# Where the score maxima of two context-attention stages read their queries and keys, and how the query stack is filled

## What is computed

```
x = x + attend(q = adaLN(x) Wq + bq, k, v = adaLN(ctx) Wkv + bkv) Wp + bp          # L0
x = x + gate_a * attend(q, k, v = modulate(LN(x)) W_qkv + b_qkv) W_proj + b_proj   # self
x = x + attend(q = LN(x) W_qc + b_qc, k, v = LN(ctx) W_kvc + b_kvc) W_cproj + ...  # cross
x = x + gate_m * (gelu(modulate(LN(x)) W_mlp1 + b_mlp1) W_mlp2 + b_mlp2)           # mlp, 2048 wide
attend = softmax(q k^T / sqrt(32)) v, for each of the 16 heads
```

## Time and profile before

| | before |
|---|---|
| time, median of 3 runs | 2688.05 us (2682.69 to 2695.44) |
| the profiled execution: its own time | 2690.8 us |
| its span, first to last instruction | 2688.9 us |
| mean granted clock of TensorE | 0.939 |
| busy shares | PE 92%, PEld 64%, DVE 51%, ACT 38%, POOL 21% |
| DMA | 349.15 MB, mean 130 GB/s |

### The profile page before, as it was taken

The page is one execution under the profiler, slowest core; times in us unless marked ns, Lnnn a source line. Parts: engine busy times, 40 slices in busy tenths (PEclk is TensorE's granted clock), DMA queues, the critical chain, the costliest instruction groups (busy, mean ns, idle before and its releaser), DMA issues. The chain is left out here.

```text
span 2688.9 us, 32715 instructions
## 1 busy us (share of the span) xinstructions
PE 2475.8 (92%) x12304; PEld 1733.0 (64%) x12304; DVE 1384.7 (51%) x2467; ACT 1028.0 (38%) x1831; POOL 575.8 (21%) x321
## 2 busy tenths in 40 slices
PE   6689899899998889999998889998999999999998
PEld 5576666568886344444444466665578888888887
DVE  4446655554445777777777556564543222222221
ACT  2524443342331455555554334333433222333231
POOL 2001111110000356666665401110110000000100
PEclk9778989899998899999999979998899999999999
DMA  6476676555556455555463477556352011101110
GB/s 225 127 191 184 192 215 178 154 164 181 183 184 181 115 129 127 150 131 131 119 152 91 140 177 204 158 163 163 105 168 75 0 56 55 55 8 48 55 40 16
DMA packets 242795, 349.15 MB, mean 130 GB/s; under 512 B 42499, under 2 KB 90715, under 8 KB 242638
## 3 DMA queue, kind: packets, MB, share of 16 engines
q1 hardware_dynamic: 241470, 343.21, 45.2%
q0 software_dynamic: 1168, 3.85, 0.4%
HBM read 228.73 MB, written 116.69 MB: 128 GB/s over the span
## 5 line engine op out<-in xcount | busy, mean ns | idle before, releaser
L1750 DVE TENSOR_REDUCE negated_max<-banks 128x1 f32<-128x512 f32 x512 | 331.4, 676 | 143.6 <-PE banks L1815 143.4
L1914 ACT ACTIVATE self_exponentials<-banks 128x512 f32<-128x512 f32 x512 | 286.6, 594 | 283.8 <-PE banks L1836 125.3
L1716 POOL TENSOR_TENSOR self_exponentials<-self_exponentials,self_exponentials 128x2048 f32<-128x2048 f32 x64 | 302.4, 4726 | 231.8 <-ACT self_exponentials L1914 231.8
L2115 PE MATMUL banks<-mlp_w_down_hi,out_parts 128*128 128x512 f32 x1024 | 333.7, 389 | 0.1
L2071 DVE TENSOR_TENSOR out_parts<-wide,out_parts 128x512 fp32r<-128x512 f32 x128 | 92.3, 721 | 372.3 <-ACT out_parts L2144 372.3
L1836 PE MATMUL banks<-self_query_stack,self_key_stack 98*128 98x512 f32 x512 | 235.8, 462 | 29.6 <-ACT self_exponentials L1914 23.1
L2134 ACT ACTIVATE wide<-banks,bias_columns 128x512 f32<-128x512 f32 x128 | 88.3, 690 | 427.3 <-PE banks L390 427.3
L1836 PEld LDWEIGHTS banks<-self_query_stack,self_key_stack 98*128 98x128 f32 x512 | 98.1, 192 | 218.5 <-ACT self_exponentials L1914 175.8
L1815 PE MATMUL banks<-self_key_stack,self_query_stack 96*128 96x512 f32 x512 | 207.6, 412 | 16.3 <-DMA self_key_stack<-k_parts_self 7.9
L334 POOL TENSOR_SCALAR norm_rstd<-norm_mean_var 128x4 f32<-128x4 f32 x32 | 8.7, 272 | 981.6 <-DVE norm_mean_var L313 981.4
L2115 PEld LDWEIGHTS banks<-mlp_w_down_hi,out_parts 128*128 128x128 f32 x1024 | 192.2, 188 | 40.4 <-DVE x_rows L1210 0.5
(11 more groups left out here) (201 smaller groups left out, 5405.0 us busy)
## 6 DMA issues: line engine op xcount, KB each, us to landing
L_query_stack<-q_parts_L SPq DMA_DIRECT2D x96, 256.0 KB, 5.8
x<-x_rows SPq DMA_DIRECT2D x24, 1024.0 KB, 4.9
norm_x<-x SPq DMA_DIRECT2D x24, 1024.0 KB, 7.3
self_query_stack<-q_parts_self SPq DMA_DIRECT2D x96, 256.0 KB, 4.0
self_key_stack<-k_parts_self SPq DMA_DIRECT2D x96, 256.0 KB, 6.2
x_rows<-x SPq DMA_DIRECT2D x24, 1024.0 KB, 5.9
cross_query_stack<-q_parts_cross SPq DMA_DIRECT2D x96, 256.0 KB, 5.7
q_parts_L<-out_parts SPq DMA_DIRECT2D x32, 512.0 KB, 3.2
```

The source lines that it names most:

```text
L1716: e.tensor_tensor(self.p[kt - 1][:], self.p[kt - 1][:], self.p[kt][:], ALU.add).then_inc(self.paired.sem, 1)
L1750: e.tensor_reduce(k.nm[n % 2][:, h * NT + t:h * NT + t + 1], k.bank[:, self.max_banks.of["max", i], :], AX_X, ALU.max, negate=True).then_i ...
L1914: e.activation(self.p[kt][:, h, :], k.bank[:, self.scores.of["score", i], :], ACT.Exp, scale=SCALE).then_inc(self.exp.sem, 1)
L2115: mm = e.matmul(bank, l, w, start=j == 0 and q == 0, stop=j == JC - 1 and q == 2)
```

## The change

Both `CrossAttention` stages are changed, and what shares memory with them.

- `fetch` and the store of queries to DRAM go. `query` on SP waits for hi, lo and the last score of group n - 4, and then issues twelve transfers from `k.outs[n % 2]` into `self.q[n % 4]`, SBUF to SBUF: four heads by hi, lo, hi, [32, 512] each (64 KB). The stack has four buffers for five.
- `maxima` reads `k.outs[n % 2]` itself, 128 rows of four heads, against block-diagonal keys: `diagonals[b % 2]`, [128, G, 2, 4 x 77], in which head h's keys stand in rows 32h to 32h + 31 and columns 77h to 77h + 76, and zeros elsewhere. A row tile takes one `product`: three matmuls of 308 columns. POOL zeroes each of the two buffers once; SP fills the blocks by eight transfers for each batch element.
- ACT's hi part of group n waits for the maxima of group n - 2 and for the twelve transfers of group n - 2, which still read the buffer. `attend` waits for the transfers and the keys.
- The lead of the queries is 4 groups for 8. The queries of groups 2 and 3 are woven with the maxima of groups 0 and 1 ahead of the loop.
- `exponentials` is a ring of six heads for eight. The bias tile, keys, values, Prepare's small tiles and the weights of Qkv and MLP get other places, with their waits; the first batch element of Qkv uses two `outs` buffers for three; the order of `Mlp.units` changes.
- Prepare gives 4 + 10 + 9 = 23 filler steps to L0 for 43, SelfAttention 35 to cross for 46.

```diff
-        self.q_parts = {s: self.dram(f"q_parts_{s}", (B, G, 2, P, N)) for s in ("L0", "self", "cross")}
+        self.q_parts = {s: self.dram(f"q_parts_{s}", (B, G, 2, P, N)) for s in ("self",)}
...
-        yield from braid(s.context(1), some(10, following))
-        yield from braid(some(14, following), after(3, splits(0, 0, 2 * G)))
-        yield from braid(s.keys(1), some(3, following))
-        yield from braid(s.values(1), some(6, following))
+        yield from braid(s.context(1), some(4, following))
+        yield from braid(some(9, following), splits(0, 0, 2 * G))
+        yield from s.keys(1)
+        yield from s.values(1)
...
-        for n in range(self.lead):
+        for n in range(2):
             yield from braid(s.query(n), quarter(n))
-            if n == self.loads_after:
-                loads()
-        yield from s.maxima(0)
-        yield from braid(s.maxima(1), after(1, s.max_rows(0)))
-        yield from braid(s.maxima(2), after(1, s.max_rows(1)))
+        s.load_diagonals(0)
+        yield from braid(s.query(2), s.maxima(0), quarter(2))
+        yield from braid(s.query(3), s.maxima(1), s.max_rows(0), quarter(3))
+        s.load_keys(0)
+        s.load_values(0)
+        yield from braid(s.maxima(2), s.max_rows(1))
+        s.load_diagonals(1)
         for n, (b, g) in enumerate(SEQ):
...
-            if n + self.FETCH < LAST:
-                s.fetch(n + self.FETCH)
+            if g == 2 and b + 2 < B:
+                s.load_diagonals(b + 2)
...
-            m = n + self.lead
+            m = n + self.LEAD
...
+        def load_diagonals(b):
+            if b == 0:
+                for done in self.context_stored[0]:
+                    sp.wait_ge(*done)
+            if b < 2:
+                sp.wait_ge(*self.diagonal_zeros(b))
+            else:
+                sp.wait_ge(*self.smax(((b - 2) * G + G - 1) * NT + NT - 1))
+            src = k_src[:, :, b * S:(b + 1) * S].rearrange("s (g h p) t -> h p g s t", h=GH, p=HD)
+            for h in range(GH):
+                for s in range(2):
+                    e.dma_start(raw(self.diagonals[b % 2][h * HD:(h + 1) * HD, :, s, h * S:(h + 1) * S]), src[h, :, :, s]).then_inc(
+                        self.d_loaded.sem(b), 16)
...
             sp.wait_ge(*self.q_hi(n))
             sp.wait_ge(*self.q_lo(n))
-            e.dma_start(q_parts[b, g].rearrange("s f t -> f s t"), raw(k.outs[n % 2][:])).then_inc(self.q_stored.sem(n), 16)
-            yield
-
-        def fetch(n):
-            b, g = SEQ[n]
-            sp.wait_ge(*self.q_stored(n))
-            if n >= 5:
-                sp.wait_ge(*self.score((n - 5) * GH + GH - 1))
+            if n >= 4:
+                sp.wait_ge(*self.score((n - 4) * GH + GH - 1))
             else:
                 for done in self.freed_q[n]:
                     sp.wait_ge(*done)
-            for r, s in enumerate((0, 1, 0)):
-                e.dma_start(raw(self.q[n % 5][r * HD:(r + 1) * HD, :, :]), q_parts[b, g, s].rearrange(
-                    "(h p) t -> p h t", p=HD)).then_inc(self.q_fetched.sem(n), 16)
+            for h in range(GH):
+                for r, s in enumerate((0, 1, 0)):
+                    e.dma_start(raw(self.q[n % 4][r * HD:(r + 1) * HD, h, :]),
+                                raw(k.outs[n % 2][h * HD:(h + 1) * HD, s, :])).then_inc(self.q_stacked.sem(n), 16)
+            yield
...
+                e.memset(raw(self.diagonals[b][:]), 0.0).then_inc(self.diagonal_zeros.sem, 1)
...
-            pe.wait_ge(*self.q_fetched(n))
-            pe.wait_ge(*self.k_loaded(b))
+            pe.wait_ge(*self.q_lo(n))
+            pe.wait_ge(*self.d_loaded(b))
...
-                for h in range(GH):
-                    mm = e.matmul(k.bank[:, bk, h * SP_:(h + 1) * SP_], self.q[n % 5][0:ST, h, t * P:(t + 1) * P],
-                                  self.keys[b % 2][0:ST, g * GH + h, :], start=True, stop=True)
-                mm.then_inc(self.smax.sem, 1)
+                whole(product(e, k.bank[:, bk, 0:GH * S], [(out[:, 0, r], out[:, 1, r], diagonals[:, g, 0, :],
+                                                            diagonals[:, g, 1, :])])).then_inc(self.smax.sem, 1)
...
         def attend(n):
             b, g = SEQ[n]
+            pe.wait_ge(*self.q_stacked(n))
             pe.wait_ge(*self.rows_put(n))
+            pe.wait_ge(*self.k_loaded(b))
...
-            o, before = k.two_outs.take(("query", self.name, n), self.q_stored(n))
+            o, before = k.two_outs.take(("query", self.name, n), self.q_stacked(n))
             act.wait_ge(*self.q_product(n))
+            if n >= 2:
+                act.wait_ge(*self.smax((n - 2) * NT + NT - 1))
...
-            o, before = k.three_outs.take(("qk", i), self.stored(i))
+            o, before = (k.two_outs if b == 0 else k.three_outs).take(("qk", i), self.stored(i))
...
-                side.append(some((1, 9, 4, 10, 10)[n - LAST], following))
+                side.append(some((1, 5, 3, 6, 8)[n - LAST], following))
```

More of the change, by code:

```diff
@@ L889 @@
     load_keys: object = nothing
+    load_diagonals: object = nothing
     load_values: object = nothing
@@ L892 @@
     add_base: object = nothing
-    fetch: object = nothing
     turn: object = idle(Norm.STEPS)
@@ L1070, in load_values @@
                     sp.wait_ge(*done)
+                for done in self.freed_v + self.freed_bias:
+                    sp.wait_ge(*done)
+                e.dma_start(self.bias_tile[:], self.bp.partition_broadcast(P)).then_inc(self.bias_loaded.sem, 16)
             if b >= 2:
@@ L1117, in project @@
             yield
-        return ContextSteps(lambda p: self.w.stage(e, sp, p + Weights.AHEAD), load_keys, load_values, load_base,
-                            fetch=fetch, turn=lambda b: self.norm.sync(e, sp, b), query=query, max_rows=max_rows,
+        return ContextSteps(lambda p: self.w.stage(e, sp, p + Weights.AHEAD), load_keys, load_diagonals, load_values,
+                            load_base, turn=lambda b: self.norm.sync(e, sp, b), query=query, max_rows=max_rows,
                             project=project)
@@ L1130, in add_base, with load_diagonals @@
                 e.tensor_tensor(k.x[:, t, :], k.x[:, t, :], self.bias_tile[:], ALU.add).then_inc(self.based.sem, 1)
-        return ContextSteps(add_base=add_base, turn=lambda b: self.norm.gpsimd(e, pool, b))
+        def load_diagonals(b):
+            if b < 2:
+                for done in self.freed_diagonals[b]:
+                    pool.wait_ge(*done)
+                e.memset(raw(self.diagonals[b][:]), 0.0).then_inc(self.diagonal_zeros.sem, 1)
+        return ContextSteps(load_diagonals=load_diagonals, add_base=add_base,
+                            turn=lambda b: self.norm.gpsimd(e, pool, b))
     def vector(self, e, dve):
@@ L1137, in load_keys @@
         def load_keys(b):
-            if b > 0:
-                return
-            for done in self.freed_kvb:
-                dve.wait_ge(*done)
-            for i in range(2):
-                e.memset(raw(self.keys[i][0:ST, :, S:SP_]), 0.0).then_inc(self.key_ones.sem, 1)
-                e.memset(raw(self.keys[i][ST:ST_MAX]), 1.0).then_inc(self.key_ones.sem, 1)
+            if b < 2:
+                for done in self.freed_keys[b]:
+                    dve.wait_ge(*done)
+                e.memset(raw(self.keys[b][ST:ST_MAX]), 1.0).then_inc(self.key_ones.sem, 1)
         def query(n):
@@ L1336, in attend @@
         def attend(n):
-            if n >= 2:
-                act.wait_ge(*self.summed(n - 2))
-            else:
-                for done in self.freed_p:
-                    act.wait_ge(*done)
             for h in range(GH):
                 i = n * GH + h
+                if i >= self.HEADS_KEPT:
+                    act.wait_ge(*self.summed((i - self.HEADS_KEPT) // GH))
+                else:
+                    for done in self.freed_p:
+                        act.wait_ge(*done)
                 act.wait_ge(*self.score(i))
-                e.activation(self.p[n % 2][:, h, :], k.bank[0:S, self.scores.of["score", i], :], ACT.Exp,
+                e.activation(self.p[:, i % self.HEADS_KEPT, :], k.bank[0:S, self.scores.of["score", i], :], ACT.Exp,
                              scale=SCALE).then_inc(self.exp.sem, 1)
@@ L1444, in begin @@
         def begin():
+            for done in self.freed_bias:
+                sp.wait_ge(*done)
             e.dma_start(self.bias_tile[:], k.a["L1_xcond_b_qkv"][2 * D:3 * D].partition_broadcast(P)).then_inc(self.bias_loaded.sem, 16)
@@ L1468, in product @@
             i, col = b * 2 * G + m, BIAS_AT["L1_b_qkv"] + m
-            o = k.outs[i % 3]
+            o = k.outs[self.slot(i)]
             dve.wait_ge(*self.hi(i))
```

147 lines of the change are left out of this document (79 added, 68 removed).

## The result

The changed kernel takes 2708.51 us (median of 6 runs, 2701.61 to 2713.83) against 2690.16 us of the kernel before in the same runs (2682.69 to 2695.44): a ratio of 1.0069, 95% interval 1.0048 to 1.0090. It is slower by 18 us, where 47 us faster were forecast: the time lies inside the stated range of 2600 to 2718, the sign is the wrong one. Its profiled execution took 2701.61 us around a span of 2699.8, so it is 7 us on the fast side of its own median.

The account below looks back on a forecast made before the run. Both context stages were taken as TensorE-bound, with a recurring stall where the query stack returns from DRAM. Terms -62.5 + 0 + 0 + 11 + 5 = -46.5 us took the profiled 2690.8 to 2644, as a median 2641; range 2600 to 2718.

Parts of the forecast that it names:

- The DRAM round trip: Cross and L0 loops: the maxima's wait for the stack fetch and the low clock behind it go, -62.5 us.
- The maxima matmuls: TensorE's score maxima: three matmuls of 308 columns replace four of 78, 0.42 us a tile against 0.46; taken as 0.
- The twelve transfers on SP: SP's queue in both context stages: copies at 0.42 us each, 8.6 of 11.2 us a group, hidden; 0.
- The new waits on SP: Loads behind the copies, such as the norm's x, come 3 us later; 0.8 us x 14 = 11 us.
- The starts: Start of both context stages: key store, zeroing, diagonal loads and landing, against context work leaving the preceding stage; +5 us.
- The rest: Six exponentials buffers, two out buffers in QKV's first element, MLP weight places and order, less DRAM traffic; 0 to +8.
- SP becomes the bound: Rival, both context stages: at 0.81 us a copy SP needs 13.3 us a group; slower, 2738 us; chance 0.15.
- paid back at the norm load: Rival: late x load holds DVE over 6 us, TensorE stops again, 3 to 4 us x 14; 2680 us; chance 0.14.
- It doesn't do what it says: Rival: clock stays low for other reasons (L0's waits for `wide`), only 36.5 us of idle go; 2668 us; chance 0.12.

Follow-up runs that it names:

- e7: Changed kernel with the query stack filled from DRAM again and the norm's x load issued ahead of the former group's query store; 2652.08 us, ratio 0.9868.
- e4: Changed kernel with four of the twelve copies a group issued by POOL, eight by SP; 2677.67 us, ratio 0.9955.
- e6: Kernel before the change, with each stack fetch from DRAM in twelve transfers of 64 KB instead of three of 256 KB; 2720.40 us, ratio 1.0132.
- e11: Changed kernel with copies only for groups 0 to 3 of each stage, other scores computed from an old stack; 2652.52 us, ratio 0.9875.
- e2: Changed kernel with the norm's x load, for elements 2 and later, issued ahead of the former group's twelve copies; 2692.05 us, ratio 1.0009.
- e9: Changed kernel with the copies of groups 0 and 1 in each stage issued behind the first load of key diagonals; 2705.39 us, ratio 1.0071.
- e1: Changed kernel with the query stack filled from DRAM again (one store, three fetches a group), block-diagonal maxima kept; 2657.43 us, ratio 0.9892.
- e12: The e7 kernel with the L0 stage's modulation (scale and shift of the normalised x) left out; 2637.56 us, ratio 0.9822.
- e3: Changed kernel with six transfers of 128 KB a group instead of twelve of 64 KB, filling the stack with wrong data; 2656.14 us, ratio 0.9879.
- e5: Changed kernel with sixteen copies a group, the third copy of each head in two halves of 32 KB; 2832.98 us, ratio 1.0543.

## Why the prediction was wrong

*The DRAM round trip (-62.5 us forecast).* Right in kind and near in size. Where SP is relieved (e7), and with the 11.0 us of queries moved in, L0's loop gains 340.9 + 11.0 - 337.0 = 14.9 us and that of cross 341.7 + 11.0 - 316.2 = 36.5. Together that is 51.4 against 62.5 - 11 for the new waits = 51.5. That closeness is luck: e7 has hardly any of the new waits, so its 51.4 stands against the 62.5, and in cross element 1 was 1.7 us longer and 2 to 4 gained 17.1 instead of 23.2. e7 also keeps the round trip: what pays is that the maxima no longer wait for it, not that it is gone.

*The maxima matmuls (0).* Right. A tile's three matmuls hold TensorE 0.43 us in cross, from 1721.29 to 1721.72 at full clock, where 0.42 was worked out and 0.46 was the old:

```profile
1721.29 0.59 PE L389 MATMUL banks<-cross_key_diagonals,out_parts 128*128 128x308 f32 x3
1721.72 0.40 PE L1278 MATMUL banks<-cross_query_stack,cross_key_stack 98*77 98x512 f32 x1
```

*The twelve transfers on SP (0, hidden).* This is the step that failed, in its price and in what was taken for hidden. The copy was priced at 0.42 us, a little over the store, "since the pattern is plain". It costs 0.62; the nearest row was the other SBUF-to-SBUF copy, at 0.57, and it was passed over. The sum was to be 8.6 of 11.2 us a group, with 2.6 to spare. Measured it is 44.9/4 = 11.2, and the gaps of about 0.1 us between the issues, which the sum leaves out, come on top: nothing to spare. But a right price alone wouldn't have turned the forecast. At 0.62 the prediction's own sum is 7.4 + 1.15 + 2.4 = 11.0 of 11.2 us, which it would still have called hidden ("below 0.64"). That a sum below the round hides is refuted: in e4 SP issues for 35 us of an element of 47.5 in cross, e6 is as far from full, and both pay. The burst delays what stands behind it, full queue or not. The price of this one term is the time of the changed kernel less e11: 56 us. The landing did hide, as worked out: a copy landed in 2.0 us. The 2.15 us that the prediction estimates from "DMA: Bandwidth & Descriptors" in the Trainium skill is close, though that section (Anatomy of one DMA) describes transfers issued by GpSimd, and these are issued by SP.

*The new waits on SP (11 us).* The mechanism was named, and so was its row to watch, but "3 us later" followed from the same 0.42. DVE waits over 5 us an element for x. The stated point, over 6 us until TensorE stops, was too high: TensorE stopped 1.2 to 1.8 us at waits of 5.1 to 5.7, and 7.7 at the 11.5 of element 1. The residual's x (the "base load") was named, but given no price; in e2 it is what TensorE waits for next. And no term held element 1, where SP is full: with its longest wait of 10.4 us in L0 and 11.5 in cross it took 8.5 and 9.1 us more than in e7, about a third of what the changed kernel loses against e7.

*The starts (+5).* Two bursts of copies stood in SP's queue ahead of Prepare's weights and key stores. The working counted stores, zeroing and diagonals, but not these, although every DMA of a moved step counts: 12.8 us ahead of L0, of which e9 got 9.1 back by moving the two bursts. In e7 nothing is lost there (171.1 + 11.0 - 182.5 = -0.4). With the 6.0 us gained ahead of cross the two starts come to +6.8, near the +5, but by luck: the 6.0 rests mostly on the short self attention of this profile.

*The rest (0 to +8).* 6.3 us between L0 and self and 6.1 at the end remain in e7. TensorE stands there 7.4 us (at 535, for the norm), where the kernel before has no such stop, and at the end 3.2 us for the norm and 7.0 for the residual (at 1894 and 1931), where that has one of 4.4 for the residual. A lead of eight had queries to cover them. That this is the cause was not tried.

*The rivals.* The first, SP becomes the bound, was right in kind and carried 0.15. Its two thresholds, 0.64 us to hide (against 11.2 us a group) and 0.75 to lose (against the average 12.5), both rest on the sum alone; at 0.62 it should have cost nothing. What was missing is the order in the queue. The second, paid back at the norm load, describes what the trace shows in cross, where elements 2 to 5 take 4.0 us more than in e7, at its price of 3 to 4 us; in L0 it shows in element 1 alone. What turns it into a loss are element 1, the starts and the ends. "It doesn't do what it says" is refuted for cross: the clock rose and elements reach 45 to 48 us in e1, e7 and e11. For L0 its reason, the waits for `wide`, was right (e12).

## What to carry to other kernels

An issuing queue is a resource with a sum and an order: add up its issue times per round, at the nearest measured price for the same pair of memories, and compare with the round that you hope for. A sum that fits isn't yet hidden: here eight copies a group, which left a fifth of the 44.7 us of an element free, still cost over 20 us (e4 against e11). Four larger transfers through DRAM beat twelve short ones inside SBUF here, since their landing was covered and the issue wasn't. When a burst is added to a queue, look at every load behind it, and in the stages before as well, for the weave may put it ahead of another stage's stores.

## What the runs showed of the hardware

- SP's time to issue a copy inside SBUF didn't go by its bytes: 0.62 us for 128 KB (e3), 0.62 for 64 KB, 0.63 for 64 and 32 KB mixed (e5), 0.58 for the 8 KB of the maximum rows. In the burst right behind the loads of x the 64 KB copies took 0.70 (8.38 us for twelve). From DRAM in bursts of twelve it was 0.49 (e6), for the store to DRAM of 512 KB 0.36. POOL issued the same copy in 0.49 (e4).
- The pair of memories doesn't settle the price either: on the way from DRAM the three transfers of the key stack took 0.99 us each in the loop (2.97 at 1721.56) and 0.50 each at the start of L0 (1.49 at 187.64), and the same store of x 0.38 in the kernel before and 0.59 behind a burst of copies. What it goes by stays open.
- In e7's L0 TensorE stood 1.47 and then 0.92 us within 4 us, and the granted clock of the next 6 us was 0.56, a mixture of the levels of 1.2 and 2.4 GHz; the same two stops in element 4 (1.45 and 0.91 us) were followed by 1.00. In e12, where TensorE stood once in each of elements 1 to 5, 1.1 to 1.8 us, the clock kept 1.00 throughout L0's elements 1 to 6.
